# An attention layer and routed experts in one kernel: new opening, an earlier table, the second bias off TensorE, later stages one tile closer, scatters 12 tiles back

## What is computed

```python
# x: (8, 512, 128), float32
x = x + attn(layernorm(x))                  # 16 heads of 8
x = x + ffn(layernorm(x))
# attn, linear and causal, no softmax:
scores = einsum('bhld,bhsd->bhls', Q, K)    # Q, K, V = ln(x) @ w.T + b
out = einsum('bhls,bhsd->bhld', scores * causal, V)
return einsum('bld,ed->ble', out, wo_w) + wo_b
# ffn: 8 experts, the 2 likeliest for each of 4096 tokens
probs = softmax(xm @ Wg); topk_p, topk_i = top_k(probs, 2)
h  = relu(xs @ W1[e] + b1[e])               # 128 -> 256
ye = h @ W2[e] + b2[e]                      # 256 -> 128
# summed over the token's two experts, each times its probability
```

## Time and profile before

| | us |
|---|---|
| three runs | 279.05, 279.58, 281.24 (median 279.58) |
| profiled execution | 280.8, its span 278.9 |
| PE busy | 224.1 (80%) |
| DVE busy | 202.9 (73%) |
| POOL busy | 206.3 (74%) |
| ACT busy | 167.7 (60%) |
| mean granted TensorE clock | 0.937 of 2.4 GHz |

### The profile page before, as it was taken

How to read it: one execution, slowest core, us unless ns; L and a number is a source line. 1 busy time by engine, 2 the same in 40 slices (tenths; PEclk the granted TensorE clock), 3 DMA queues, 4 the chain that set the end, 5 groups by cost and what they waited for, 6 DMA issues and landing times.

```text
span 278.9 us, 6531 instructions
## 1 busy us (share of the span) xinstructions
PE 224.1 (80%) x1396; PEld 166.4 (60%) x1396; DVE 202.9 (73%) x689; ACT 167.7 (60%) x655; POOL 206.3 (74%) x194
## 2 busy tenths in 40 slices
PE   6799799999888989888782159999999999997000
PEld 2444466655555545454452049999999999996000
DVE  7869999999979798797988576455455546555903
ACT  2454268989677686775765636677676665674000
POOL 3287279878989898898977777777777777777730
PEclk9999999999999999999998559999999999999655
DMA  6970000000110001010012375343433334377745
GB/s 167 295 212 0 4 0 0 4 21 20 38 33 29 29 29 42 20 38 30 30 48 87 115 163 157 99 124 93 108 103 90 95 105 119 77 260 280 216 126 183
DMA packets 31174, 25.72 MB, mean 92 GB/s; under 512 B 4856, under 2 KB 28033, under 8 KB 31138
## 3 DMA queue, kind: packets, MB, share of 16 engines
q1 hardware_dynamic: 22550, 14.75, 19.5%
q0 software_dynamic: 4352, 8.47, 9.2%
q10 hardware_dynamic: 4236, 2.10, 2.8%
HBM read 13.54 MB, written 12.27 MB: 93 GB/s over the span
## 4 chain that ended last, share of the span: by engine, by line
PE 53%; POOL 19%; issue 9%; DVE 8%; ACT 5%; DMA 2%; POOLq 1%; DVEq 1%; ACTq 1%; SPq 0%
PE ps L1044 14%; PE ps L1054 11%; PE ps L951 11%; POOL outer L437 9%; POOL dispatched L465 7%; PE ps L913 4%; POOL returned L474 3%; PE ps L1035 3%; PE ps L1001 2%; PE ps L959 1%; PE ps L1056 1%; DMA back<-returned 1%; DVE prod L682 1%; PE ps L962 1%; PE ps L915 1%
## 5 line engine op out<-in xcount | busy, mean ns | idle before, releaser
L474 POOL DMA_INDIRECT returned<-y_sb,xt x72 | 71.7, 995 | 21.9 <-issue 14.9
L437 POOL TENSOR_TENSOR outer<-qkv 128x1024 f32<-128x1024 f32 x32 | 62.6, 1957 | 21.1 <-ACT qkv L553 20.6
L465 POOL DMA_INDIRECT dispatched<-rows,slot x64 | 62.7, 979 | 16.9 <-issue 14.5
L951 PE MATMUL ps<-outer,causal 128*128 128x512 f32 x128 | 62.7, 612 | 9.4 <-POOL outer L437 9.4
L887 DVE TENSOR_SCALAR y_sb<-ps,xt 128x128 f32<-128x128 f32 (+1 forms) x80 | 28.0, 350 | 41.1 <-PE ps L1056 39.6
L1044 PE MATMUL ps<-xT,back 128*128 128x128 f32 (+1 forms) x320 | 52.4, 292 | 1.0 <-ACT xT L603 0.8
L1054 PE MATMUL ps<-w_sb,hT 128*128 x320 | 48.7, 278 | 0.0
L611 ACT ACTIVATE hT<-ps,b_col 128x128 f32<-128x128 f32 (+1 forms) x160 | 47.2, 357 | 0.7 <-PE ps L1044 0.7
L682 DVE TENSOR_TENSOR prod<-ps,qkv 128x1024 f32<-128x1024 f32 x32 | 39.0, 1219 | 10.1 <-PE ps L951 9.9
L1044 PEld LDWEIGHTS ps<-xT,back 128*128 128x128 f32 x320 | 42.6, 197 | 3.0 <-ACT xT L603 2.0
L1054 PEld LDWEIGHTS ps<-w_sb,hT 128*128 128x128 f32 x320 | 42.3, 193 | 0.5 <-issue 0.2
(11 more groups left out here) (156 smaller groups left out, 362.6 us busy)
## 6 DMA issues: line engine op xcount, KB each, us to landing
xt<-dispatched SPq DMA_DIRECT2D x64, 65.0 KB, 1.9
back<-returned SPq DMA_DIRECT2D x8, 512.0 KB, 7.2
x_sb<-x SPq DMA_DIRECT2D x8, 256.0 KB, 5.0
out<-x_sb ACTq DMA_DIRECT2D x8, 256.0 KB, 2.4
dispatched<-padding SPq DMA_DIRECT2D x18, 65.0 KB
returned<-y_sb,xt POOLq DMA_INDIRECT x72, 2.4
w_sb<-w SPq DMA_DIRECT2D x1, 1024.0 KB, 6.6
w_sb<-w SPq DMA_DIRECT2D x2, 512.0 KB, 7.5
```

The lines of the kernel that those rows point to most:

```text
L437: pool.tensor_tensor(outer[:, g % OUTER_RING, :].rearrange("p (h b a) -> p h b a", h=HEADS, b=DH), k, v, ALU.mult).then_inc(outer_done, 1)
L465: pool.indirect_dma_start(out=dispatched[:, :], out_offset=bass.IndirectOffsetOnAxis(ap=slot[:, g * K + k:g * K + k + 1], axis=0), in_=row ...
L474: pool.indirect_dma_start(out=returned[:, :], out_offset=bass.IndirectOffsetOnAxis(ap=xt[:, n % G, D:D + 1].bitcast(I32), axis=0), in_=y_s ...
L951: mm = pe.matmul(ps_run[g % 2][:, u, :], causal[:, :], outer[:, g % OUTER_RING, 512 * u:512 * (u + 1)], start=True, stop=True)
```

## The change

The later stages come one slot closer on TensorE, VectorE and ScalarE: from `o_transposed` (7 to 6) on, with `q_transposed` (5 to 4). `dispatch` goes from 14 slots back to 12. `split_bias` and the third matmul of the experts are gone; `b2` is loaded to all partitions beside `b1`, ScalarE multiplies its row with the probability (`b2_out`), and VectorE adds it in the instruction that scales. `first_table` moves from VectorE's slot 34 to slot 30. In the opening `ones` is filled second, the warming matmuls are 7, the gate's bias is done in slot 0 on TensorE and VectorE, and the statistics of batches 4 to 7 go to slots 1, 3, 5, 7.

```diff
-    STATE_AFTER = 5
-    FIRST_TABLE_AFTER = 3
+    STATE_AFTER = 4
+    FIRST_TABLE_AFTER = -1
...
-    WARM = (10, 3)
+    WARM = 7
...
-            sp.dma_start(b1_col[:, :], b1).then_inc(w_ffn, 16)
+            sp.dma_start(biases[:, :, D:D + HC], b1.rearrange("p (e c) -> p e c", e=E)).then_inc(w_ffn, 16)
+            sp.dma_start(biases[:, :, 0:D], bcast(b2.rearrange("(e d) -> e d", e=E))).then_inc(w_ffn, 16)
...
-            tile_slots([(14, dispatch), (0, outer_product), (0, split_bias)], N)
+            tile_slots([(12, dispatch), (0, outer_product)], N)
...
-                if g == 11:
+                if g == 13:
                     deviation1(3)
...
-            tile_slots([(10, variance_log2), (10, scale2_out), (10, negative_mean2), (10, exponentials), (2, qkv_out), (11, probabilities),
-                        (1, xnT_out), (6, qT_out), (10, shift2_out), (10, rows_out), (0, normalize), (7, oT_out), (0, deviations_ahead)], N)
+            tile_slots([(9, variance_log2), (9, scale2_out), (9, negative_mean2), (9, exponentials), (2, qkv_out), (10, probabilities),
+                        (1, xnT_out), (5, qT_out), (9, shift2_out), (9, rows_out), (0, normalize), (6, oT_out), (0, deviations_ahead)], N)
...
+            def b2_out(n):
+                wait(act, y_done, pieces(n + 1 - W))
+                for i, entry in enumerate(entries(n)):
+                    part = rows_of(n, i)
+                    act.activation(b2_of[part, n % W, :], bias_flat[part, bass.ds(bias_at[entry], D)], ACT.Identity,
+                                   scale=xt[part, n % G, D + 1:D + 2]).then_inc(b2of_done, 1)
+
+            tile_slots([(1, xT_out), (3, hT_out), (3, b2_out), (-3, bias_registers)], BLOCKS)
...
+            dve.memset(ones[:, :], 1.0).then_inc(bias_done, 1)
...
-            dve.memset(b2_rows[:, :], 0.0).then_inc(b2_step, 1)
-            dve.memset(b2_parts[:, :], 0.0).then_inc(b2_step, 1)
...
-                if 0 < g <= B - 4:
-                    mean1_out(g + 3)
+                if g in (1, 3, 5, 7):
+                    mean1_out(4 + g // 2)
                 if g == 3:
                     scale1_out(2)
-                if g == 9:
+                if g == 11:
                     scale1_out(3)
...
-            tile_slots([(2, gate_bias), (6, stats2_out), (6, mean2_out), (5, add_residual), (5, softmax_start), (7, softmax_end), (1, attend_sum),
-                        (0, attend), (0, scales_ahead), (7, places),
+            tile_slots([(0, gate_bias), (5, stats2_out), (5, mean2_out), (4, add_residual), (4, softmax_start), (6, softmax_end), (1, attend_sum),
+                        (0, attend), (0, scales_ahead), (6, places),
                         (2, state_out), (FIRST_TABLE_AFTER, first_table)], N)
...
-                    dve.tensor_scalar(y_sb[part, n % G, :], ps_y[n % 2][part, i, :], xt[part, n % G, D + 1:D + 2], None,
-                                      ALU.mult).then_inc(y_done, 1)
+                    dve.scalar_tensor_tensor(out=y_sb[part, n % G, :], in0=ps_y[n % 2][part, i, :], scalar=xt[part, n % G, D + 1:D + 2],
+                                             in1=b2_of[part, n % W, :], op0=ALU.mult, op1=ALU.add).then_inc(y_done, 1)
...
-            keep_busy(WARM[0])
+            keep_busy(WARM)
...
-            tile_slots([(3, running_sums), (5, q_transposed), (7, o_transposed), (5, sum_state), (1, project),
-                        (0, transpose1), (7, project_out), (10, rank), (0, warm), (2, gate_weights)], N)
+            tile_slots([(3, running_sums), (4, q_transposed), (6, o_transposed), (5, sum_state), (1, project),
+                        (0, transpose1), (6, project_out), (9, rank), (0, gate_weights)], N)
...
-                    mm = pe.matmul(ps_y[n % 2][:, i, :], ones[:, :], b2_parts[:, bass.ds(w2_from[entry], D)], start=False, stop=True)
```

More of the change, by code:

```diff
@@ L340, in _ @@
                              w2[:, c * P:(c + 1) * P, :].rearrange("e p d -> p e d")).then_inc(w_ffn, 16)
-            sp.wait_ge(b2_step, 1)
-            for part in range(3):
-                sp.dma_start(b2_rows[32 * part:32 * part + 1, :], b2.rearrange("(one n) -> one n", one=1)).then_inc(b2_in, 16)
             sp.wait_ge(consts, N_CONSTS)
@@ L597, in bias_registers @@
                     act.wait_ge(table_done[1 if n >= SPLIT.start else 0], 5)
-                    bias_at.update(zip(own, read(mybir.EngineType.Activation, b1_at[0:1, own.start:own.stop], (E - 1) * HC)))
+                    bias_at.update(zip(own, read(mybir.EngineType.Activation, b1_at[0:1, own.start:own.stop], (E - 1) * (D + HC))))
             def xT_out(n):
@@ L830, in table @@
                 dve.wait_ge(step, 18)
-                for at, each in ((w1_at, H), (b1_at, HC), (w2_at, D)):
+                for at, each in ((w1_at, H), (b1_at, D + HC), (w2_at, D)):
                     dve.tensor_scalar(at[:, own], expert_f[:, own], float(E - 1), float(each), ALU.min, ALU.mult).then_inc(done, 1)
@@ L883, in y_out @@
                 wait(dve, y_mm, n + 1)
+                wait(dve, b2of_done, pieces(n + 1))
                 wait(dve, return_done[n % G], 16 * (n // G))
```

50 lines of the change are left out of this document (12 added, 38 removed).

## The result

The changed kernel takes **283.29 us**, median (282.52 to 284.84), against 279.74 for the kernel before beside it: ratio 1.0119 with a 95% interval of 1.0086 to 1.0152. It is slower by a little over 1%; the forecast was 277.7 with a range to 280.3. The profiled execution took 284.59 us, with a span of 282.8.

The account below looks back on a forecast made before the run. GpSimd was taken to bound 208 us of the span, TensorE before that. Terms -3.1, -2.2, +0.7, -0.5 and +3.3 put the first return 1.9 us sooner: 277.7 us against the median 279.58, range 274.3 to 280.3.

Parts of the forecast that it names:

- Scatters 12 back, -3.1: GpSimd: scatters start after tile 11's outer product, without the old wait and bias split; first return 3.1 us sooner.
- 1 to spare, nothing is added: First scatter: slots of tiles 0 to 3 ready about 49 us, wanted at 50.3, so no wait.
- Rival 4: VectorE bounds before the scatters: late state or places, or first scatter waits; 279.9 us, chance 0.12.
- Statistics and gate bias, -2.2: VectorE: spread statistics and earlier gate bias remove TensorE's 2.23 us wait for tile 1's state; 2.2 us gained.
- closer stages, +0.7: TensorE up to tile 11's projection: one more transposition with state part and one more output projection; 0.7 us lost.
- the wait I named: TensorE's 2.23 us wait for `state` of tile 1, which VectorE wrote late behind another batch's statistics; expected to go.
- Opening, -0.5: TensorE's start: fewer warming matmuls, gate products first; projection at 9.0 to 9.2 instead of 9.51, 0.5 us gained.
- Rival 3: TensorE stays slow in the opening, first sums and a projection taking twice as long, about 2 us; 279.7, chance 0.13.
- E: Start of GpSimd's first bare scatter, one without an outer product between; 139.20 us before, forecast at 139.1.
- First table, +3.3: Early table on VectorE delays slots of tiles 24 to 27; GpSimd waits 3.3 us after eight bare scatters, ends 0 and 4.2.
- Second bias, 0: Experts: bias moves from TensorE to ScalarE and VectorE, about 1.1 us per ScalarE block, covered by GpSimd's 1.29; 0 us.
- Rival 2: ScalarE bounds the experts at 1.35 us per block; last return 5 to 6 us late, 283 us, chance 0.09.

Follow-up runs that it names:

- lag_14: Changed kernel with scatters 14 tiles back as before instead of 12, the first table left early: 282.32 us, ratio 1.0077 to the kernel before.
- before_lag12_2: Second run of the kernel before with only the scatter lag changed, 12 tiles back instead of 14: ratio 1.0179 to the kernel before.
- opening_back: Changed kernel with the old beginning: ten warming matmuls and three more, gate products in slot 2 on TensorE and VectorE: 282.23 us, ratio 1.0068.
- gate_slot2: Changed kernel with the gate products back in slot 2 on TensorE and VectorE, seven warming matmuls kept: ratio 0.9952 on a slower chip.

## Why the prediction was wrong

Its frame held: GpSimd is back to back in all its long stretches but one, and the sum over its starts gives the time. Two terms and one wait failed, all to the slow side; what the forecast had at -1.9 for the first return came out at +3.5.

- **Scatters 12 back, -3.1: right.** Without its wait the first scatter is 2.1 us behind the start of the outer product of tile 11 instead of 9.0, two slots more, four bare scatters less; lag_14 shows the same trade from the other side.
- **"1 to spare, nothing is added": wrong by 1.0.** The slots of tiles 0 to 3 were written at 52.27, not 49, just as GpSimd was ready, and another 1.00 us passed between `slot` and the scatter, which the forecast had at nothing. The first scatter waited 1.1 to 1.4 us in every kernel with a lag of twelve. Before, the slots stood at 54.62 (before_lag12_2: first scatter at 55.62). Rival 4 named this.
- **Statistics and gate bias, -2.2, closer stages, +0.7: right as a sum.** From the first outer product to that of tile 11 it takes 38.34 us before and 36.98 in opening_back, which has the closer stages and the spread statistics, but the old warming and the old place of the gate's bias: -1.4 for -1.5. The share of each is not separated; the spreading of the statistics alone gave 0.8 to 1.0, and not by the wait I named.
- **Opening, -0.5: the first step that failed.** I looked at when the first projection starts (9.34, for 9.0 to 9.2) and took the pace behind it as given. Rival 3 was the case, though the projection is not late: the slow pace lasts to 17 us, and from the first outer product, which starts where it did before, to that of tile 11 it takes 38.26 us instead of opening_back's 36.98: +1.3 for -0.5. opening_back gives 2.2 at E and 1.4 us in the time back, gate_slot2 rules out the gate's products, and the shorter warming is left. The same projection takes 1.67 us and then 0.82, a factor of two like that of the two levels. The forecast said that the granted clock reads full in both paces; the trace has no clock record before the first rise, and where lag_14 has one it is 1.2 GHz in the slow stretch. The rule of the Trainium skill that I cited (TensorE: Matmul & The Clock Gate, The HAM clock gate) has the array at the lower level until it has been kept busy, and these durations agree with it.
- **First table, +3.3: the term that was mis-sized, measured +6.0.** The mechanism and the place were right (one gap, after the eighth bare scatter, ended by what waits for `slot`). E + 13.4 became E + 15.3: the table ended 1.0 later, because `prod` of tile 30 was not done at E - 0.8 but at E + 0.25, and 0.96 was VectorE's wait for TensorE, which had stood idle for the table and was at the lower clock; which of the two made it late is not separated. The last 0.8 is the time between `slot` and the scatter, left out here as for the first scatter. I had counted one engine's queue, and left out that its neighbours stop with it and that a result isn't used at the moment it is written.
- **Second bias, 0: right.** Rival 2 did not come. The last `y_sb` before is written at 256.63, not 256.28, where it starts, so the lead was 10.4 us and not 10.8; it is 14.3 now, since the returns are late and not the experts.

The sum of what was measured: -3.1 + 1.0 - 1.4 + 1.3 + 6.0 - 0.2 (slots of 4.43 instead of 4.437) = +3.6 us at the first return, where 3.5 are to be explained. In the final time the ratio gives 3.3. My chance of 0.07 for slower by over 1% was too low for another reason too: I let the rivals stand one at a time, and two of them (3 and 4) came together with a term beyond its bad end (6.0 us, where I had 4.2).

## What to carry to other kernels

An edit that moves a long serial piece of work earlier in one in-order queue is priced by the other queues: list who waits for what stands behind it, and who waits for those. Shortening a lag takes the slack that such a piece lived on, so price the two together; in front of tile 24 the short lag alone opened no gap, the early table alone 1.2 us, both 6.3. A gap that is closed can come back behind: the later table cost 2.7 us in front of tile 28. Add the time from the end of an instruction to the start of what waits for it, here 0.8 to 1.0 us from VectorE to a scatter, and check a named releaser against the program. And judge a warming-up by the durations of the work behind it, not by when that work starts.

## What the runs showed that I had not expected

One kind of VectorE instruction, when it falls beside a GpSimd outer product, ends with it. In the changed kernel the scales of a batch (128x8 elements, from SBUF to SBUF) take 1.58 us; in opening_back, where no outer product is under way, 0.13:

```profile
27.60 1.95 POOL L427 TENSOR_TENSOR outer<-qkv 128x1024 f32<-128x1024 f32 x1 [1.26 <-ACT qkv L529]
27.99 1.58 DVE L633 SCALAR_TENSOR_TENSOR norm<-mv,norm 128x8 f32<-128x8 f32 x1
29.50 0.28 DVE L671 TENSOR_TENSOR state<-ps,headmask 128x128 f32<-128x128 f32 x1
29.83 0.49 PE L944 MATMUL ps<-qT,state 128*128 128x128 f32 x2 [0.33 <-DVE state L671]
```

```profile
25.16 1.95 POOL L427 TENSOR_TENSOR outer<-qkv 128x1024 f32<-128x1024 f32 x1 [1.26 <-ACT qkv L529]
27.24 0.13 DVE L633 SCALAR_TENSOR_TENSOR norm<-mv,norm 128x8 f32<-128x8 f32 x1
```

27.99 + 1.58 = 29.57 is the end of the outer product, 27.60 + 1.95 = 29.55, to 0.02 us. In the kernel before the same instruction took 0.89 at 13.04, to 13.93, and the outer product ended at 13.91. `prod` and `o_sb`, which run beside outer products all the time, keep their 1.2 us. Behind the late scales stood `state` of tile 1, 29.50, for which TensorE waited 0.33 us. In the twenty traces 18 such instructions (128x4 to 128x16) fell beside an outer product, and all ended 0.01 to 0.04 us after it. Four more, in the kernels that still split the bias, ended the same way with L454 (in before 49.43 and 49.41). The other 58, with neither under way, took 0.12 to 0.17 us. No run changed this instruction alone, so the cause is read from such coincidences and not shown.
